# An attention and butterfly-FFN layer on one core: a reordered head, an fp32r first FFN layer, and the row maxima transposed by VectorE

## The reference

```python
# x [4,1024,128], 16 heads of 64; w_q, w_k, w_v, w_o [128,16,64]
def attn(x):
    q, k, v = (einsum('BSE,EHK->BSHK', x, w) for w in (w_q, w_k, w_v))
    logits = einsum('BSHK,BMHK->BSHM', q, k) / 8 + causal_mask
    return einsum('BSHK,EHK->BSE', softmax(logits) @ v, w_o)
def ffn(x):
    h = butterfly(x @ W_exp + b_exp, up_weights, 512)      # 9 stages of 2x2 rotations
    h = gelu(h + up_bias)                                  # the exact form
    return butterfly(h, down_weights, 512) @ W_con + b_con + down_bias
x = layernorm(x + attn(x))
x = layernorm(x + ffn(x))
```

## Time and profile before

| | us |
|---|---|
| median of 3 runs | 1051.42 (1051.22 to 1052.35) |
| the profiled execution | 1050.42 |
| its span, first to last instruction | 1048.5 |
| TensorE busy | 1014.8 (97%) |
| VectorE busy | 753.1 (72%) |
| GpSimd busy | 757.2 (72%) |
| ScalarE busy | 602.8 (57%) |
| chain that ended last: TensorE's share | 91% |

### The profile page before, as it was taken

The page is one execution under the profiler, slowest core; times in us unless marked ns, Lnnn a source line. Parts: engine busy times, 40 slices in busy tenths (PEclk is TensorE's granted clock), DMA queues, the critical chain, the costliest instruction groups (busy, mean ns, idle before and its releaser), DMA issues.

```text
span 1048.5 us, 17665 instructions
## 1 busy us (share of the span) xinstructions
PE 1014.8 (97%) x5816; PEld 697.7 (67%) x5816; DVE 753.1 (72%) x2013; ACT 602.8 (57%) x1214; POOL 757.2 (72%) x725
## 2 busy tenths in 40 slices
PE   4799999999999999999999999999999999999997
PEld 3556667676667766767666766676666676665576
DVE  6666777677677777776778777877777778773446
ACT  4355566665566565666666656666555655664431
POOL 6278877777779777777778877777777887777322
PEclk9699999999999999999999999999999999999999
DMA  7112223223131223232232222332313212220002
GB/s 222 44 45 67 59 58 82 63 82 79 45 81 42 73 52 83 62 82 62 64 80 55 63 58 53 82 82 63 81 43 81 68 47 72 62 62 22 22 19 63
DMA packets 45800, 68.69 MB, mean 66 GB/s; under 512 B 15079, under 2 KB 21515, under 8 KB 45710
## 3 DMA queue, kind: packets, MB, share of 16 engines
q1 hardware_dynamic: 45710, 67.57, 25.2%
HBM read 31.11 MB, written 2.36 MB: 32 GB/s over the span
## 4 chain that ended last, share of the span: by engine, by line
PE 91%; DMA 3%; DVE 2%; POOL 2%; issue 1%; SPq 1%; ACT 0%; POOLq 0%; DVEq 0%; ACTq 0%
PE O L691 25%; PE WORK L616 14%; PE SC L666 13%; PE SC L670 12%; PE WORK L631 5%; PE WORK L653 3%; PE WORK L753 3%; PE WORK L594 3%; PE WORK L592 3%; PE WORK L593 3%; PE WORK L602 1%; PE WORK L604 1%; PE WORK L603 1%; PE SC L741 1%; PE WORK L741 1%; DMA R<-RROW 1%
## 5 line engine op out<-in xcount | busy, mean ns | idle before, releaser
L836 ACT ACTIVATE PR<-SC 128x512 f32<-128x512 f32 (+3 forms) x768 | 354.9, 490 | 278.2 <-PE SC L670 251.9
L493 POOL TENSOR_TENSOR SUM<-SUM,PR 128x1024 f32<-128x1024 f32 (+3 forms) x256 | 418.9, 1636 | 14.9 <-POOL SUM L502 0.5
L960 DVE CUSTOM_DVE_ANT_0 WORK<-WORK,CMASK 128x128 f32<-128x128 f32 (+3 forms) x512 | 239.1, 513 | 65.9 <-PE WORK L616 65.8
L666 PE MATMUL SC<-QH,KHL 128*128 128x512 f32 (+3 forms) x768 | 271.9, 359 | 4.8 <-ACT PR L836 3.2
L670 PE MATMUL SC<-QL,KH 128*128 128x512 f32 (+3 forms) x768 | 262.8, 346 | 0.0
L478 POOL TENSOR_SCALAR_AFFINE_SELECT PR<-PR 128x256 f32<-128x256 f32 x256 | 105.8, 415 | 206.1 <-ACT PR L836 205.9
L616 PE MATMUL WORK<-KHL,QH 128*128 128x512 f32 (+3 forms) x768 | 225.1, 361 | 5.4 <-DMA KH<-KHL 4.0
L691 PE MATMUL O<-PR,VLO 128*64 128x512 f32 (+3 forms) x1024 | 200.0, 522 | 1.2 <-DVE OT L1030 1.0
L666 PEld LDWEIGHTS SC<-QH,KHL 128*128 128x128 f32 x768 | 145.2, 189 | 63.8 <-ACT PR L836 29.2
L616 PEld LDWEIGHTS WORK<-KHL,QH 128*128 128x128 f32 x768 | 135.8, 191 | 56.0 <-issue 35.3
L963 DVE TENSOR_REDUCE MP<-WORK 128x1 f32<-128x512 f32 x256 | 164.2, 683 | 4.7
(11 more groups left out here) (100 smaller groups left out, 1070.5 us busy)
## 6 DMA issues: line engine op xcount, KB each, us to landing
QH<-QH SPq DMA_DIRECT2D x128, 128.0 KB, 2.3
KH<-KHL SPq DMA_DIRECT2D x128, 128.0 KB, 2.3
R<-RROW SPq DMA_DIRECT2D x64, 256.0 KB, 3.9
SW<-in_L_ffn_up_weights_dram SPq DMA_DIRECT2D x9, 512.0 KB, 4.6
SW<-_L_ffn_down_weights_dram SPq DMA_DIRECT2D x9, 512.0 KB, 4.4
out_dram<-X SPq DMA_DIRECT2D x8, 256.0 KB, 2.3
X<-in_L_attn_x_BSE_dram SPq DMA_DIRECT2D x1, 512.0 KB, 4.6
WQKV<-in_L_attn_w_q_dram SPq DMA_DIRECT2D x1, 512.0 KB, 5.4
```

The costliest lines, as they stand in the source:

```text
L493: nc.gpsimd.tensor_tensor(total, total, prob(unit, s), ALU.add).then_inc(add_done, 1)
L666: nc.tensor.matmul(dst, KHL[:, par, h, kt * P:(kt + 1) * P], QH[:, par, h, q0:q0 + n], start=True, stop=False)
L836: nc.scalar.activation(prob(unit, s)[:, h, :], SC[use % NSC][:, 0:n], ACT.Exp, scale=K ** -0.5).then_inc(exp_done, 1)
L960: op = nc.vector.tensor_tensor_reduce(cols, cols, CMASK[:, CH - n:], 1.0, LOWEST, ALU.add, ALU.max, cell)
```

## The change

- **Loads.** SP loads the first half of x's batch 0, then only the weight columns of the first unit (128 of w_q and w_k, 256 of w_v), then the second half. The rest of the weights comes after the bias rows. W_exp and batch 1 of x are issued before `rows(0)`, batches 2 and 3 in units 0 and 1. w_o, W_con and the biases are issued before the wait for `blocks_done`, into other places (OT, R, SUM, SW, W2).
- **Head.** Only the two lays of batch 0 stay ahead of the projections. Batch 1 is laid in units 0 to 3; w_o, the bias column and W_con become fillers in units 1, 0 and 0 (`ONCE_AT`).
- **Maxima.** `mt` is gone. VectorE transposes the four 32x32 blocks of NEGM (now 128x32) into NROW (now 32x128, float32) right after L967.
- **FFN.** `up` is three fp32r passes per tile. W1 is split at step 8 of the last window; the x1 groups are split by ScalarE and VectorE into the idle half of QH, QL, KHL and KH1. DOWN_LAG is 4. The first two tiles of `up(0)` stand ahead of the last norm. In the last window recip and scale come one step earlier.
- **End.** The last group is treated as two pieces of two tiles. From piece 3 on the result is made by ScalarE as x RSTD + SHIFT, SHIFT = -mean RSTD from two more GpSimd instructions per piece.

```diff
-DOWN_LAG = 3
+DOWN_LAG = 4
-FILL[10] = [[("mt",)], [("proj", 0, 0)], []]
+FILL[10] = [[], [("proj", 0, 0)], []]
+ONCE_AT = {("wo", 0): (1, 3, 2), ("wo", 1): (1, 6, 2), ("bias", 0): (0, 9, 2), ("con", 0): (0, 10, 2)}
-LAST_SCALE = 4
+LAST_RECIP, LAST_SCALE = 1, 3
+FFN_PIECES = [(g * TPC, (g + 1) * TPC) for g in range(B * CHUNKS - 1)]
+FFN_PIECES += [(B * TILES - TPC, B * TILES - 2), (B * TILES - 2, B * TILES)]
+ACT_RESULTS = 3
+W1_SPLIT_AT = (UNITS - 1, 8)
-    if 0 < b < B - 1 and n < LAY_UNITS:
+    if b < B - 1 and n < LAY_UNITS:
...
# sync
-            sp.dma_start(X[:, 0:TILES, :], x_tiles[:, 0:TILES, :]).then_inc(in_x[0], 16)
-            for n, w in enumerate((w_q, w_k, w_v)):
-                sp.dma_start(WQKV[:, n, :], w.rearrange("e h k -> e (h k)")).then_inc(in_w, 16)
+            sp.dma_start(X[:, 0:TPC, :], x_tiles[:, 0:TPC, :]).then_inc(in_x[0], 16)
+            weights = [w.rearrange("e h k -> e (h k)") for w in (w_q, w_k, w_v)]
+            first = [P, P, 2 * P]
+            for n, w in enumerate(weights):
+                sp.dma_start(WQKV[:, n, 0:first[n]], w[:, 0:first[n]]).then_inc(in_first, 16)
+            sp.dma_start(X[:, TPC:TILES, :], x_tiles[:, TPC:TILES, :]).then_inc(in_x[1], 16)
...
-            sp.dma_start(X[:, TILES:, :], x_tiles[:, TILES:, :]).then_inc(in_x[1], 16)
+            for n, w in enumerate(weights):
+                sp.dma_start(WQKV[:, n, first[n]:], w[:, first[n]:]).then_inc(in_w, 16)
...
             copies(0)
             sp.sem_inc(sums_landed, 16)
-            sp.wait_ge(blocks_done, 1)
-            sp.dma_start(BROW, BLOCKS).then_inc(brow_in, 16)
...
+            sp.wait_ge(blocks_done, 1)
+            sp.dma_start(BROW, BLOCKS).then_inc(brow_in, 16)
+            sp.dma_start(W1[:, :], W_exp).then_inc(in_exp, 16)
+            sp.dma_start(X[:, TILES:2 * TILES, :], x_tiles[:, TILES:2 * TILES, :]).then_inc(in_x[2], 16)
             rows(0)
...
# vector, at the last maximum
                         nc.vector.tensor_reduce(NEGM[:, 0:2 * TILES], MP[:, :, :], AX_X, ALU.max,
                                                 negate=True).then_inc(negm_made, 1)
-                elif f[0] == "mt":
-                    dve.wait_ge(work_ready, at + 1)
-                    if u >= 0:
-                        dve.wait_ge(m_landed, (u + 1) * 16)
-                    nc.vector.tensor_copy(NROW[:, :], w[0:2 * TILES, 0:P]).then_inc(nrow_made, 1)
+                        dve.wait_ge(negm_made, u + 2)
+                        if u >= 0:
+                            dve.wait_ge(m_landed, (u + 1) * 16)
+                        for b in range(0, P, BLK):
+                            op = nc.vector.transpose(NROW[:, b:b + BLK], NEGM[b:b + BLK, :])
+                        op.then_inc(nrow_made, 1)
...
# tensor
-            norm(take_work(LAST_NORM), UNITS - 1)
-            pe.wait_ge(exp_done, UNITS * 2 * NS + EXP_CREDIT)
...
-                    nc.tensor.matmul(hid_banks[t_], W1[:, t_ * P:(t_ + 1) * P], x1T[g % EARLY_GROUPS], start=True,
+                    nc.tensor.matmul(hid_banks[t_], W1H[:, rows], x1_hi_slots[g], start=True, stop=False)
+                    nc.tensor.matmul(hid_banks[t_], W1L[:, rows], x1_hi_slots[g], start=False, stop=False)
+                    nc.tensor.matmul(hid_banks[t_], W1H[:, rows], x1_lo_slots[g], start=False,
                                      stop=True).then_inc(hid_ready, 1)
...
-            for g in range(DOWN_LAG):
+            pe.wait_ge(exp_done, UNITS * 2 * NS + EXP_CREDIT)
+            up(0, range(2))
+            norm(take_work(LAST_NORM), UNITS - 1)
+            up(0, range(2, HT))
+            for g in range(1, DOWN_LAG):
                 up(g)
...
# gpsimd, per piece of the FFN
+                if n >= ACT_RESULTS:
+                    pool.wait_ge(rstd_made, B + n + 1)
+                    nc.gpsimd.tensor_tensor(SHIFT[:, first:end], MV[:, first:end, 0], RSTD[:, first:end],
+                                            ALU.mult).then_inc(shift_mult, 1)
+                    pool.wait_ge(shift_mult, n - ACT_RESULTS + 1)
+                    nc.gpsimd.tensor_scalar(SHIFT[:, first:end], SHIFT[:, first:end], -1.0, None,
+                                            ALU.mult).then_inc(shift_made, 1)
# scalar, after the last Gelu
+            for n in range(ACT_RESULTS, len(FFN_PIECES)):
+                act.wait_ge(shift_made, n - ACT_RESULTS + 1)
+                for t in range(*FFN_PIECES[n]):
+                    nc.scalar.activation(X[:, t, :], X[:, t, :], ACT.Identity, scale=RSTD[:, t:t + 1],
+                                         bias=SHIFT[:, t:t + 1]).then_inc(act_out_made, 1)
```

More of the change, by code:

```diff
@@ L228, in post_norm_layer @@
         HALF = sb("HALF", [P, B * TILES])
+        SHIFT = sb("SHIFT", [P, B * TILES])
         W1 = sb("W1", [P, HID])
@@ L357, in stage_weights @@
                     sp.wait_ge(composed, 3 * n)
+                else:
+                    sp.wait_ge(bc_made, 1)
                 w, st = (up_w, n) if n < STAGES else (down_w, 2 * STAGES - 1 - n)
@@ L426, in _ @@
                 sp.wait_ge(dup_landed[c], 64 * UNITS)
[L428 to L432, removed]
+            for n, (first, end) in enumerate(FFN_PIECES):
+                if n < ACT_RESULTS:
+                    sp.wait_ge(out_made, end)
+                else:
+                    sp.wait_ge(act_out_made, end - FFN_PIECES[ACT_RESULTS][0])
+                sp.dma_start(out_tiles[:, first:end, :], X[:, first:end, :]).then_inc(out_stored, 16)
+            sp.wait_ge(out_stored, 16 * len(FFN_PIECES))
         @block.gpsimd
@@ L636, in filler @@
                         t = nc.tensor.transpose(w[:, i * P:(i + 1) * P], X[:, f[1] * TPC + i, :], IDN[:])
+                elif f[0] == "wo":
+                    pe.wait_ge(in_wo, 16)
+                    for i in range(TPC):
+                        pr = f[1] * TPC + i
+                        t = nc.tensor.transpose(w[:, i * P:(i + 1) * P], wo_nat[:, pr * P:(pr + 1) * P], IDN[:])
+                elif f[0] == "con":
+                    pe.wait_ge(in_con, 16)
+                    for i in range(HT):
+                        t = nc.tensor.transpose(w[:, i * P:(i + 1) * P], wcon_nat[:, i, :], IDN[:])
+                elif f[0] == "bias":
+                    pe.wait_ge(brow_made, 1)
+                    for i in range(HT):
+                        t = nc.tensor.matmul(w[:, i:i + 1], BROW[:, i * P:(i + 1) * P], ONES[0:1, 0:1], start=True, stop=True)
                 elif f[0] == "w2":
@@ L1000, in consume @@
                     add_bc(g)
+                elif f[0] == "wo":
+                    dve.wait_ge(work_ready, at + 1)
+                    nc.vector.tensor_copy(WOT[:, f[1] * TPC:(f[1] + 1) * TPC, :],
+                                          w[:, :].rearrange("p (t d) -> p t d", t=TPC)).then_inc(free, 1)
+                elif f[0] == "con":
+                    dve.wait_ge(work_ready, at + 1)
+                    nc.vector.tensor_copy(w2t, w[:, :]).then_inc(con_copied, 1)
+                    dve.wait_ge(con_copied, 1)
+                    dve.sem_inc(free, 1)
+                elif f[0] == "bias":
+                    dve.wait_ge(in_bc, 32)
+                    nc.vector.tensor_tensor(BC[:, :], BC[:, :], down_row, ALU.add).then_inc(bc_made, 1)
+                    dve.wait_ge(work_ready, at + 1)
+                    nc.vector.tensor_copy(BIAS1[:, :], w[:, 0:HT]).then_inc(free, 1)
+                    dve.wait_ge(bc_made, 1)
                 elif f[0] == "w2":
```

221 lines of the change are left out of this document (102 added, 119 removed).

## The result

| | before | after | ratio, 95% interval |
|---|---|---|---|
| median, us | 1051.87 (4 runs, 1051.22 to 1052.35) | 1036.99 (4 runs, 1035.7 to 1037.28) | 0.9857 [0.9839, 0.9874] |
| the profiled execution | 1050.42 | 1035.7 | |
| its span | 1048.5 | 1033.9 | |

The change takes 14.9 us off. The forecast was 1035.4, within 1030 to 1042. A cut is the start of the first QL pass of a unit, so the trace gives each number to 0.01 us.

What follows compares the result with a forecast made beforehand. TensorE bounds the long middle; VectorE is nearly full in part of the head. Head -10.5, moved work +2.9, NEGM transposes -3.5, FFN -4.7, end 0 sum to -15.8 us: 1035.4 us, range 1030 to 1042.

Steps and rivals of the forecast that it cites:

- Earlier start: Head: smaller first loads of x and weights start the first projection at about 7.5 us, not 10.39: -2.9 us.
- Rival (b): Head bounded elsewhere, by slow weight slices and queued copies: first score 7 us earlier, not 10.5; 1039 us, chance 0.14.
- The rest of the head: Head: lay copies gone 3.0 us, idle before WOT 1.4, NEGM to NROW 0.4, bias matmuls and BIAS1 copy 2.8.
- The moved work: Units 0 to 3: lays, w_o, W_con and bias put there as 28 TensorE instructions cost +2.9 us (1.5 to 5).
- The NEGM transposes in the loop: Units 0 to 30: 31 TensorE transposes of 0.115 us removed, 3.5 us gone (0 to 4.5).
- VectorE's transposes: Maxima: each 32x32 transpose on VectorE taken as 0.1 us; the four may take 2.4 us before TensorE waits.
- Rival (a): Loop: VectorE transposes wait for GpSimd adds; one wait per unit 1047.5 us, two 1122; chance 0.03 each.
- The FFN: FFN: twelve fp32r passes per group save 5.1 us; last matmul 4.7 us earlier, last window's 0.4 included (-2.5 to -6).
- two prices for the table load: Before up(1): Gelu table load 1.4 us in all by the trace, or 2.66 with the skill's 1.38 us drain.
- The end: After the last matmul: GpSimd's three last pieces queue, 7.7 us against 7.6, so 0 (-1.5 to +1.5).
- c: Rival: nothing gained from the NEGM transposes, and the moved work costs 5 us; 1041 us, chance 0.08.
- d: Rival: a better tail, with no queue on GpSimd and no stall; 1032.5 us, chance 0.12.

Runs made afterwards that it cites:

- experiment 3: Kernel after, but w_q, w_k and w_v loaded whole before the second half of x: 1040.31 us, ratio 0.9893 to the kernel before.
- Experiment 1: Kernel before, with only NEGM's TensorE transpose and VectorE's cast replaced by four 32x32 VectorE transposes: 1049.72 us, ratio 0.9977.
- experiment 6: Kernel after, with the bias column moved to step 11 of unit 0 and both w_o transposes to step 11 of unit 1: 1036.13 us, ratio 0.9871.
- experiment 2: Kernel after, with 12 spare VectorE transposes of NEGM's blocks ahead of the four that count: 1084.5 us, ratio 1.031 to the kernel before.
- experiment 11: Kernel after, with w_o and bias blocks in the head's wait, Gelu table loaded earlier, ScalarE's results for pieces 3 to 6 alone: 1030.96 us, ratio 0.9799.
- experiment 7: Kernel after, with all results normalised by VectorE, each piece's right behind the next one's residual: 1035.4 us, ratio 0.9852 to the kernel before.
- experiment 4: Kernel after, with the last norm ahead of all of up(0): 1036.66 us, ratio 0.9856 to the kernel before.
- experiments 9: Kernel after, with both w_o blocks and the bias block moved from units 0 and 1 into the head's wait for the row: 1033.43 us, ratio 0.9825.

## Why the prediction was right

The time was within 1.6 us of the forecast, and no term had the wrong sign. One term came out for another reason than was given, and misses of 3.7 us in all left 1.2. By its own steps:

- **Earlier start: right.** 2.9 us forecast, 3.3 measured (10.39 to 7.07), and experiment 3 gives back 3.6 at the first score. Rival (b), a head bounded elsewhere, falls by it.
- **The rest of the head: right, and 0.4 more.** The lay copies and the idle time before WOT were to give 4.4 us: the maxima's stretch went from 16.4 to 12.0. NEGM to NROW gave nothing (0.87 us now, 0.92 before); from NEGM to the first QL pass it is 5.91 before and 2.97 after, 2.9 less where 3.2 were forecast. This number is nearly right, but not by the reason given. The forecast put 2.8 us down to the eight bias passes and the BIAS1 copy. Experiment 1 keeps both and has 3.57 us: 2.3 of the 2.9 us came without moving them, most of it because the early projection no longer waits for NEGM behind `mt`, a path that the forecast didn't name, and part of it by the clock. What moving the bias work can have brought is the other 0.6. Another 0.7 us came from the way between first projection and first maximum (10.29 to 9.61), of which the forecast said nothing.
- **The moved work: undersized.** Against experiment 1, which has the transposes too, it costs 3.4 us in units 0 and 1 and 0.3 in units 2 and 3: 3.7, not 2.9. The forecast counted issue distances alone. In unit 0 the clock adds to it: it is 0.50 until 36.4 us after, 4.8 us of the unit, and for 3.1 us of unit 0 in experiment 1, 2.6 before. The w_o blocks also take VectorE's time in unit 1, and a v block waits for it (0.33 us). That nothing waits on SyncE's moved DMAs held only while the addition to BC came early (experiment 6).
- **The NEGM transposes in the loop: right in kind, oversized.** Forecast 3.5 us. With 3.7 for the moved work, units 0 to 30, longer by 1.3 in all, leave 2.3 to 2.4 for them. This split is good to 1 us or so, because units 4 to 30 took 786.9 to 789.2 us in profiled kernels whose loop is the same. The median unit gained 0.09 us where 0.115 had been read from two starts around one transpose; the rest went into single units that wait, as in experiment 1.
- **VectorE's transposes: 0.21 us each, not 0.1.** It costs nothing, since 0.84 us lie within the slack of 2.4, as experiment 2 shows. Rival (a) falls in both forms: none of 128 transposes waited for GpSimd, though 112 ran inside one of its adds. The half of the Trainium skill's rule (SBUF — State Buffer, Who interferes with whom) on one SBUF input outside the two-port modes fits these rows. So does its other half: the low part of W1, with two SBUF inputs, took 2.73 us on VectorE, beside a GpSimd add that ended at 957.48, where the same size from PSUM takes 0.68. The forecast named it, and TensorE did not wait for it. VectorE's timeline, then GpSimd's:

```profile
953.01 0.68 DVE L928 TENSOR_TENSOR KHL<-WORK,QH 128x512 fp32r<-128x512 f32 x1
...
955.30 2.73 DVE L928 TENSOR_TENSOR WSV<-W,WST 128x512 fp32r<-128x512 f32 x1
```

```profile
954.86 2.62 POOL L517 TENSOR_TENSOR SUM<-SUM,PR 128x1024 f32<-128x1024 f32 x1
```

- **The FFN: right.** Passes start 0.23 us apart, the 0.95 us wait for OT is gone, and TensorE stalls 1.17 us for the Gelu where 1.2 were forecast. Of the two prices for the table load the trace has the shorter: 1.28 us, 0.10 behind the copy, 0.02 ahead of the Gelu. -4.2 against -4.7: from `up(1)` to the last matmul's start it is 52.6 us where it was 56.9, 4.3 less, and what is missing is the last window's 0.4. From its first QL pass to `up(1)` it is 35.3 us, and 35.2 before. No run takes the fp32r passes back by themselves, so their share is read from the trace alone.
- **The end: within the stated bounds, 0.4 better.** GpSimd does queue to the end, as forecast, but with 1.73 us per piece of two tiles (1027.37 to 1029.10) and not 1.8, and smaller instructions of 0.20 to 0.25 us. The end shrank by 0.4.
- **Two slips in the arithmetic.** 1034.6 plus 1.0 is 1035.6 and not 1035.4. The chances of the cases that are faster (the forecast, b, c, d, and a with one wait at 1047.5) add up to 0.95 and not 0.94. Neither changes the verdict.

The terms were off by 0.9 in the head, -0.8 and -1.1 in the units, -0.5 in the FFN and 0.4 at the end (plus is more gain than forecast). The gains of 1.3 us cancel half of the 2.4 us that are missing, so the total is closer than the terms, and that is luck.

## What to carry to other kernels

Work moved off a busy start should go into a wait that stays, not into a loop where the engine is full: in the 2.8 us in which TensorE waited for the row, the same blocks cost nothing. When an instruction moves, look at what other queues wait for it, above all a DMA queue. The last piece of a kernel belongs to the engine that can finish it with the fewest hand-overs. This holds for the last pieces alone (two in experiment 11): when VectorE got all of them, the queue moved there (experiment 7). When an instruction is taken out, look also at what stood behind it in the same queue: dropping `mt` freed a projection that had waited with it.

## What the runs showed of the hardware

- VectorE's 32x32 float32 transpose takes 199 to 205 ns in 128 instances of the kernel after, and 0.21 us from start to start.
- The DMA that spreads R lands 3.9 us after issue in the median, but up to 4.7 us in experiment 1 and 5.1 in experiment 4. Units of experiment 1 were up to 0.8 us longer.
- ScalarE's Identity with scale and bias per partition takes 0.41 us per 128x128 tile in a row of four (1.65), 0.48 by itself. VectorE's normalisation takes 0.27 in a row of four (1.08) and 0.30 in a row of two (0.60).
- A VectorE instruction with two inputs from SBUF took 2.73 us beside a GpSimd add, and 0.68 with one input from PSUM; a 32x32 transpose beside such adds never took longer than 0.205.
- TensorE's granted clock stood at 1.00 through the head's end where the wait for the row was filled with matmuls (experiments 9 and 11), and at 0.50 to 0.79 in the nine executions with TensorE idle there.
